# The opening of a one-core transformer layer: other fills on GpSimd, half of the queries cleared by ScalarE, the first products ordered by parts

## Chip, core and metric

The kernel runs on one core of one Trainium2 chip. The metric is the device time of one execution in microseconds (us), the median over several runs. A core has five engines with instruction streams of their own, which meet only at semaphores: TensorE (PE in the rows; its weight loads are PEld), VectorE (DVE), ScalarE (ACT), GpSimd (POOL) and SyncE (SP), which here only issues transfers.

## What is computed

The reference is a layer with two halves over `x` of 8 batches by 512 tokens by 256 channels. Cut to what the opening touches, it is:

```
xn = layernorm(x)                                  # rows: (x - mean) / sqrt(var + eps)
q, k, v = split(xn @ w_qkv.T)                      # 16 heads of 16
s = softmax(q @ k.T / 4 + causal) @ v @ w_out.T
g = silu((silu(xn @ wg.T) * (xn @ wu.T)) @ wd.T)   # 768 hidden columns
x = x + s * g
# second half: layernorm, a long convolution, a mixture of 20 experts, and x = x + s * silu(y)
```

## The kernel before, in words

Everything is one program with the order of each engine's work written out by hand and semaphores between the engines. The first half of the layer runs batch by batch (`sequence(b)` on every engine): batches 1 to 6 are a loop, batch 0 and the last are written out. Ahead of batch 0 stands the opening, the only place that the change touches: weights are loaded and converted, tiles that need constants are filled, batch 0 is normalised, projected and taken half-way through its gated hidden layer.

Products are made nearly exact with numbers cut in two parts, a high one (`HI`, rounded) and a low one (`LO`, what was lost). ScalarE writes the high part, VectorE or GpSimd subtracts it from the number and writes the low part. A projection is six products for each 128 output columns: three pairs of parts (`PAIRS`) by two halves of the 256 channels (`c`).

In the opening the engines do this:

- SyncE (`load_x`, `load_weights`) issues the loads of `x`, of the weights and of small tables, then `load_x(1)` when batch 0 is normalised, then writes the parts of queries and keys to memory (`spill`) and reads them back in the layout of the attention (`stack`, four groups of four heads). `stack` waits until the tiles `qs` and `ks` of its group have been filled.
- VectorE fills `nothing` and two of four groups of `qs` with zeros (`clear_queries`), does the first normalisation (`norm(0, NORM_X)`: statistics, variance, and in `norm_rows` four row tiles of `xn`), writes the low parts of `Wqkv` and of `xnT`, converts `Wgu`, writes the low parts of queries and keys (`split_qk`) with the other two clears between them, writes the low part of `Wg1`, multiplies the first three (`EARLY`) blocks of the hidden layer (`gated`), and does the second normalisation, `norm(1, NORM_X)`, for batch 1. Then it enters `sequence(0)`, which begins with `gated(0, 3)`.
- GpSimd builds masks, fills the four groups of `ks` with zeros and `V` with ones, and sets two rows of each group of `ks` to one (L1852). Between the second and the third group it raises the variance to the power of -1/2 (`power`), on which the rows of `xn` wait.
- TensorE transposes `xn` (L831), makes the four query and key tiles (`project_qk`, products at L822), the gate and up products of blocks 0 and 1 (`gate_up`), the values (`project_v`), block 2, and in `sequence(0)` blocks 3 to 5, batch 1's transposes, the down products (`down`, L904) and the scores (`unit`, L999). The gate and up products of block 3 wait for `v_sb` (the values kept), those of blocks 4 and 5 for `gated` of blocks 2 and 3.
- ScalarE converts weights, writes the high parts, and for each hidden block takes the SiLU of the gate (`silu_of_gate`, tile `sil`) and the high part of the product (`hidden`); GpSimd writes the low part of that product (`hidden_low`). `keep_v` copies the values into `V`.

The two lines that matter most for the order on VectorE ahead of `gated(0, 3)` and on TensorE ahead of block 5:

```
elif i >= 4:
    pe.wait_ge(S["h32_sb"], NF * b + i - 1)      # gate_up: block 5 waits for gated(0, 3)
...
norm(1, NORM_X)                                   # VectorE, then sequence(0): gated(0, 3)
```

Of the kernel before, what the change touches and what calls it, by code (L numbers as in the profile page):

```python
# [54 lines left out]
def program(nc, x, wqkvT, woutT, wguT, wdT, wg1, bg1, wg2, bg2, winT, bin_, short, wo2, bo2, fw1, fb1, fw2, fb2,  # L55
# [15 lines left out]
    with ctx:  # L71
# [210 lines left out]
        def f(ap):  # L282

            return ap.bitcast(F32)
# [295 lines left out]
        rest_in = sem("rest_in"); w_ms = sem("w_ms"); k_zero = sem("k_zero"); k_set = sem("k_set"); q_zero = sem("q_zero")  # L580
# [84 lines left out]
        def attention_sync(sp):  # L665
# [116 lines left out]
            for g in range(NG):  # L782
                sp.wait_ge(k_set, g + 1)
                sp.wait_ge(q_zero, g + 2)
                stack(0, g)
# [29 lines left out]
        def attention_tensor(pe):  # L815
# [18 lines left out]
            def project_qk(b, tiles):  # L834

                for m in tiles:
                    if m == 0:
                        pe.wait_ge(S["xnT_hi"], b + 1)
                        pe.wait_ge(S["xnT_lo"], b + 1)
                        at_least(pe, S["g_sb"], 2 * b)  # L840
                    if m >= 2:
                        pe.wait_ge(S["qk_lo"], 4 * b + m - 1)
                    o = C * (m % 2) + P * (m // 2)
                    split_products(PS[:, m % 2, :],
                                   lambda i, c: Wqkv[:, i, c, o:o + P],
                                   lambda j, c: xnT[:, j, c, :]).then_inc(S["qk_ps"], 1)

# [318 lines left out]
            pe.wait_ge(qkv_lo, 1)  # L1166
            project_qk(0, range(4))
# [27 lines left out]
        def attention_scalar(act):  # L1195
# [5 lines left out]
            def split_qk(b):  # L1201
                for m in range(4):
                    if m == 0:
                        at_least(act, S["on_sb"], NT * (b - 1))
                        at_least(act, S["ont"], b - 1)
                    act.wait_ge(S["qk_ps"], 4 * b + m + 1)
                    dst = khl if m % 2 else qhl
                    act.activation(dst[:, m // 2, HI, :], PS[:, m % 2, :], ACT.Copy).then_inc(S["qk_hi"], 1)
# [147 lines left out]

            act.wait_ge(qkv_in, 16)
            act.activation(Wqkv[:, HI, :, :], st_qkv[:, :, :], ACT.Copy).then_inc(qkv_hi, 1)
            split_x(0)
            act.wait_ge(d_in, 16)  # L1360
            act.activation(Wd[:, :, :], st_d[:, :, :], ACT.Copy).then_inc(d_sb, 1)
            split_qk(0)
            act.wait_ge(g1_in, 16)
# [3 lines left out]
            for i in range(EARLY):  # L1367
                if i == 0:
                    act.wait_ge(gu_sb, 1)
                    act.wait_ge(qkv_lo, 1)  # L1370
                    act.wait_ge(g1_lo, 1)
                silu_of_gate(0, i)
                hidden(0, i)
            act.wait_ge(v_ones, 1)
            act.wait_ge(rest_in, REST)
            keep_v(0)
# [17 lines left out]
        def attention_vector(dve):  # L1394
# [350 lines left out]
            split_qk(0, (0,))  # L1745
            clear_queries(2)
            split_qk(0, (1,))
            clear_queries(3)
            split_qk(0, (2, 3))
# [3 lines left out]
            for i in range(EARLY):  # L1753
                gated(0, i)
# [21 lines left out]
        def attention_gpsimd(pool):  # L1776
# [58 lines left out]

            pool.memset(neghalf[:, :], -0.5)
            pool.memset(mask16[:, :], 0.0).then_inc(w_ms, 1)
# [6 lines left out]
            for g in range(NG):  # L1844
                if g == 2:
                    power(0, veps, rstd, "ln_var", "ln_std")
                pool.memset(f(ks[:, GH * g:GH * g + GH, :]), 0.0).then_inc(k_zero, 1)
            pool.memset(V[:, :, :, :], 1.0).then_inc(v_ones, 1)
            pool.wait_ge(k_zero, NG)
            pool.wait_ge(v_ones, 1)  # L1850
            for g in range(NG):
                pool.memset(f(ks[M0:M0 + 2, GH * g:GH * g + GH, :]), 1.0).then_inc(k_set, 1)  # L1852
            pool.wait_ge(k_set, NG)
# [439 lines left out]
```

## Time and profile before

| | us |
|---|---|
| median of 3 runs | 1057.13 |
| lowest and highest run | 1054.28 and 1058.62 |
| span of the profiled execution, first to last instruction | 1027.7 |
| median less span | 29.4 |
| busy in the span: PE / DVE / ACT / POOL | 939.8 / 699.9 / 464.7 / 350.3 |
| mean granted TensorE clock (1.00 is 2.4 GHz, 0.50 is 1.2 GHz) | 0.968 |

The profiled execution has no time of its own beside its span; the 29.4 us between its span and the median of the runs lie before the first and behind the last instruction. All times below count from the first instruction of the span. TensorE is busy for 91% of the span, but does nothing in its first 19.7 us; the opening, up to the first scores of batch 0, takes the first 57 us.

### The profile page before, as it was taken

How to read it: one execution, taken by the hardware profiler on the slowest of the kernel's cores; microseconds unless marked ns; L12 is line 12 of the kernel's file. 1: busy time of each engine (PE TensorE's matmuls, PEld its weight loads, DVE VectorE, ACT ScalarE, POOL GpSimd, SP SyncE). 2: the span in 40 equal slices, each digit the busy share in tenths (PEclk: the TensorE clock that was granted, in tenths of full speed). 3: DMA queues.
4: the chain of work that ended last, by engine and by line, in shares of the span. 5: the costliest groups of instructions: out<-in, count | busy, mean ns of one | idle time of the engine just before them, and what ended most of it. 6: DMA issues, size and time to landing. Idle time of an engine off the chain costs nothing.

```text
span 1027.7 us, 18869 instructions
## 1 busy us (share of the span) xinstructions
PE 939.8 (91%) x5808; PEld 713.4 (69%) x5808; DVE 699.9 (68%) x1451; ACT 464.7 (45%) x869; POOL 350.3 (34%) x609
## 2 busy tenths in 40 slices
PE   1999999999999999999999999985798998999996
PEld 1776776776776686686686676564566677888885
DVE  8565477577577677667667566545375437999998
ACT  2435546546536636636636644633232334443441
POOL 7203313613623622532532451343000018833320
PEclk9988999999999999999999998988899999999999
DMA  5774854644634633733634630067767653544421
GB/s 184 157 159 80 161 190 66 123 150 80 115 133 96 117 139 87 117 131 91 104 115 112 103 128 22 2 217 224 253 218 229 212 185 115 164 129 141 144 86 41
DMA packets 88186, 136.68 MB, mean 133 GB/s; under 512 B 9987, under 2 KB 63939, under 8 KB 86084
## 3 DMA queue, kind: packets, MB, share of 16 engines
q1 hardware_dynamic: 69636, 100.75, 40.2%
q10 hardware_dynamic: 12352, 18.48, 5.3%
q0 software_dynamic: 6144, 16.79, 5.3%
q8 instruction: 27, 0.44, 0.2%
q14 instruction: 27, 0.22, 0.1%
HBM read 79.36 MB, written 55.57 MB: 131 GB/s over the span
## 4 chain that ended last, share of the span: by engine, by line
PE 38%; issue 29%; POOL 15%; DVE 10%; ACT 3%; DMA 2%; SPq 1%; POOLq 0%; DVEq 0%; ACTq 0%
PE PS L1980 7%; POOL PT L1800 6%; POOL slots_in L661 4%; PE PS L314 4%; PE PS L822 4%; PE PS L370 3%; PE PS L999 3%; POOL h L1783 3%; PE PS L1027 3%; PE PS L1041 3%; PE PS L337 2%; PE PS L405 2%; PE PS L1963 2%; POOL idle_p L1794 2%; DVE xn L1426 1%
## 5 line engine op out<-in xcount | busy, mean ns | idle before, releaser
L1510 DVE TENSOR_REDUCE Mneg<-PS 128x2 f32<-128x1024 f32 (+2 forms) x192 | 195.1, 1043 | 66.0 <-PE PS L1003 64.8
L1270 ACT ACTIVATE PT<-PS 128x512 f32<-128x512 f32 (+1 forms) x384 | 172.6, 529 | 118.1 <-PE PS L1027 116.2
L1794 POOL TENSOR_TENSOR idle_p<-neghalf 128x1 f32<-128x1 f32 x128 | 25.2, 197 | 304.0 <-ACT PT L1270 304.0
L999 PE MATMUL PS<-ks,qs 96*128 96x256 f32 (+3 forms) x512 | 121.5, 347 | 3.1 <-issue 2.1
L1027 PE MATMUL PS<-qs,ks 96*128 96x512 f32 (+3 forms) x512 | 121.1, 355 | 2.4 <-ACT PT L1270 1.3
L1027 PEld LDWEIGHTS PS<-qs,ks 96*128 96x128 f32 x512 | 88.1, 193 | 36.2 <-ACT PT L1270 18.1
L822 PE MATMUL PS<-xnT,Wgu 128*128 128x512 f32 x384 | 102.9, 409 | 2.9 <-ACT V L1215 2.4
L1980 PE MATMUL PS<-Wes,xbT 128*128 x336 | 99.0, 405 | 3.3 <-issue 2.6
L1800 POOL TENSOR_SCALAR_AFFINE_SELECT PT<-PT 128x256 f32<-128x256 f32 x256 | 99.0, 410 | 0.0
L1041 PE MATMUL PS<-PT,V 128*32 128x512 f32 (+3 forms) x1024 | 89.1, 455 | 5.4 <-POOL PT L1800 4.3
L822 PEld LDWEIGHTS PS<-xnT,Wgu 128*128 128x128 f32 x384 | 69.9, 191 | 25.8 <-issue 7.2
L999 PEld LDWEIGHTS PS<-ks,qs 96*128 96x128 f32 x512 | 77.5, 197 | 14.5 <-issue 9.1
L2203 POOL DMA_INDIRECT yg<-slots_out,pos x64 | 77.9, 1217 | 18.9 <-issue 17.9
L2038 DVE TENSOR_TENSOR yb<-PS,bes 128x256 f32<-128x256 f32 x84 | 35.2, 423 | 61.1 <-PE PS L1980 47.7
L1783 POOL TENSOR_TENSOR h<-h,h 128x512 fp32r<-128x512 f32 x40 | 51.3, 1290 | 62.0 <-ACT h L1234 61.8
L2002 ACT ACTIVATE xbT<-PS 128x256 f32<-128x256 f32 x84 | 31.4, 384 | 87.2 <-PE PS L1963 67.5
L1980 PEld LDWEIGHTS PS<-Wes,xbT 128*128 128x128 f32 x336 | 54.0, 196 | 23.4 <-issue 20.4
L661 POOL DMA_INDIRECT slots_in<-xn,rows_now x64 | 62.4, 974 | 17.5 <-issue 17.0
L1453 DVE SCALAR_TENSOR_TENSOR h<-PS,sil 128x512 f32<-128x512 f32 x48 | 32.5, 688 | 47.7 <-ACT sil L1227 36.4
L370 PE MATMUL PS<-Inv,Z 128*128 128x256 f32 x256 | 61.0, 393 | 3.0 <-DVE Z L519 2.5
L1003 PE MATMUL PS<-mask,ident 128*128 128x128 f16 (+2 forms) x352 | 63.6, 256 | 0.0
L314 PE MATMUL PS<-v,Fwd 128*128 128x256 f32 x432 | 57.1, 293 | 2.8 <-issue 2.8
(233 smaller groups left out, 1600.3 us busy)
## 6 DMA issues: line engine op xcount, KB each, us to landing
qs<-qk_parts SPq DMA_DIRECT2D x96, 128.0 KB
ks<-qk_parts SPq DMA_DIRECT2D x96, 128.0 KB
slots_out<-yb ACTq DMA_DIRECT2D x28, 384.0 KB, 3.1
xb<-slots_in SPq DMA_DIRECT2D x83, 128.0 KB, 2.6
qk_parts<-qhl SPq DMA_DIRECT2D x16, 512.0 KB, 2.7
qk_parts<-khl SPq DMA_DIRECT2D x16, 512.0 KB, 3.1
xn2T_parts<-xn2T SPq DMA_DIRECT2D x8, 1024.0 KB, 4.9
xT<-xn2T_parts ACTq DMA_DIRECT2D x7, 1024.0 KB
```

Of the source, the lines that this page charges most:

```text
L314: last = pe.matmul(PS[:, bank, C * (q_ % 2):C * (q_ % 2) + C], Fwd[:, i, kc, P * q_:P * q_ + P], src[:, j, 2 * half + kc, :], start=n == 0 ...
L370: last = pe.matmul(PS[:, 6 + m, C * z:C * z + C], Z[:, z, c, P * m:P * m + P], Inv[:, c, :], start=c == 0, stop=c == NQ - 1)
L661: pool.indirect_dma_start(slots_in, bass.IndirectOffsetOnAxis(rows_now[:, t, k:k + 1], axis=0), xn2[:, t, :], None).then_inc(S["sent"], 16)
L822: last = pe.matmul(out, lhs(i, c), rhs(j, c), start=last is None, stop=n == 0)
L999: pe.matmul(out, qs[:, hd, P * qt:P * qt + P], ks[:, hd, 0:keys], start=n % a_bank == 0, stop=False, skip_group_check=True)
L1027: last = pe.matmul(PS[:, 4 + n, col:col + T - P * kt], ks[:, hd, P * kt:P * kt + P], qs[:, hd, P * kt:T], start=True, stop=True)
L1041: last = pe.matmul(PS[32 * j:32 * j + 32, 7, P * kt:T], V[:, kt, GH * g + j, :], PT[:, g % 2, j, COL[kt]:COL[kt] + T - P * kt], start=kt = ...
L1270: act.activation(PT[:, g % 2, j, 512 * n:512 * n + width], PS[:, 4 + n, 0:width], ACT.Exp, scale=SCALE).then_inc(S["exped"], 1)
L1510: dve.tensor_reduce(out=Mneg[:, 0, qt, heads[0]:heads[-1] + 1], in_=all_of, op=ALU.max, axis=AX.X, negate=True).then_inc(S["maxed"], 1)
L1783: pool.tensor_tensor(h[:, i, LO, :], h32[:, i % 2, :], f(h[:, i, HI, :]), ALU.subtract).then_inc(S["h_lo"], 1)
L1800: last = pool.affine_select(out=blocks, in_=blocks, compare_op=ALU.is_ge, fill=0.0, base=0, pattern=[[0, 2], [1, P]], channel_multiplier=-1)
L1980: ins = pe.matmul(PS[:, HALF + u % HALF, 0:C], xbT[:, u, c, :], Wes[:, bass.ds(expert, 1), c, :].rearrange("p o n -> p (o n)"), start=c == ...
```

## The change

It leaves the arithmetic as it is and changes only which engine fills which tile, in which order, and the order of the six products of each of batch 0's query and key tiles.

- GpSimd: a group of `ks` is filled with ones at once (`keys_of_ones`) in the place of a fill with zeros and a second one of two rows with ones; the rows between are multiplied by zeros of `qs`. Two groups come first, then `power`, then a wait until all four row tiles of `xn` are written, and only then the other two groups, `V` and the masks.
- ScalarE clears groups 2 and 3 of `qs` at its very start; VectorE no longer does.
- TensorE's first four tiles use `project_qk_first`: high by high first, then low weights by high `xnT`, then high weights by low `xnT`, each with a wait of its own.
- ScalarE's order: the conversion of `Wd` goes from ahead of the query and key splits to behind `keep_v`; `keep_v` goes ahead of block 2; the high part of `Wg1` and `ident16` go behind the three early blocks. VectorE's low part of `Wg1` goes behind them too.

```
@@ attention_sync
-                sp.wait_ge(k_set, g + 1)
-                sp.wait_ge(q_zero, g + 2)
+                sp.wait_ge(k_ones, g + 1)
+                if g < 2:
+                    sp.wait_ge(q_zero, g + 2)
+                else:
+                    sp.wait_ge(q_cleared, g - 1)
                 stack(0, g)
@@ attention_tensor
+            def project_qk_first(m):
+                o = C * (m % 2) + P * (m // 2)
+                if m >= 2:
+                    pe.wait_ge(S["qk_lo"], m - 1)
+                n = 0
+                for i, j in ((HI, HI), (LO, HI), (HI, LO)):
+                    if m == 0 and i == j:
+                        pe.wait_ge(S["xnT_hi"], 1)
+                        pe.wait_ge(qkv_hi, 1)
+                    if m == 0 and i == LO:
+                        pe.wait_ge(qkv_lo, 1)
+                    if m == 0 and j == LO:
+                        pe.wait_ge(S["xnT_lo"], 1)
+                    for c in range(CC):
+                        last = pe.matmul(PS[:, m % 2, :], Wqkv[:, i, c, o:o + P], xnT[:, j, c, :],
+                                         start=n == 0, stop=n == 5)
+                        n += 1
+                last.then_inc(S["qk_ps"], 1)
...
-            pe.wait_ge(qkv_lo, 1)
-            project_qk(0, range(4))
+            for m in range(4):
+                project_qk_first(m)
@@ attention_scalar
+            act.wait_ge(q_zero, 1)
+            for g in (2, 3):
+                act.activation(qs[:, GH * g:GH * g + GH, :].rearrange("p h t -> p (h t)"),
+                               nothing[0:KS, 0:1].to_broadcast([KS, GH * T]), ACT.Copy).then_inc(q_cleared, 1)
             act.wait_ge(qkv_in, 16)
             act.activation(Wqkv[:, HI, :, :], st_qkv[:, :, :], ACT.Copy).then_inc(qkv_hi, 1)
             split_x(0)
-            act.wait_ge(d_in, 16)
-            act.activation(Wd[:, :, :], st_d[:, :, :], ACT.Copy).then_inc(d_sb, 1)
             split_qk(0)
+            for i in range(EARLY):
+                if i == 0:
+                    act.wait_ge(gu_sb, 1)
+                    act.wait_ge(qkv_lo, 1)
+                if i == 2:
+                    act.wait_ge(v_ones, 1)
+                    keep_v(0)
+                    act.wait_ge(d_in, 16)
+                    act.activation(Wd[:, :, :], st_d[:, :, :], ACT.Copy).then_inc(d_sb, 1)
+                    act.wait_ge(d_sb, 1)
+                silu_of_gate(0, i)
+                hidden(0, i)
             act.wait_ge(g1_in, 16)
             act.activation(Wg1[:, HI, :, :], st_g1[:, :, :], ACT.Copy).then_inc(g1_hi, 1)
...
-            for i in range(EARLY):
-                if i == 0:
-                    act.wait_ge(gu_sb, 1)
-                    act.wait_ge(qkv_lo, 1)
-                    act.wait_ge(g1_lo, 1)
-                silu_of_gate(0, i)
-                hidden(0, i)
-            act.wait_ge(v_ones, 1)
+            act.wait_ge(g1_lo, 1)
             act.wait_ge(rest_in, REST)
-            keep_v(0)
@@ attention_vector
-            split_qk(0, (0,))
-            clear_queries(2)
-            split_qk(0, (1,))
-            clear_queries(3)
-            split_qk(0, (2, 3))
+            split_qk(0, range(4))
+            for i in range(EARLY):
+                gated(0, i)
             dve.wait_ge(g1_hi, 1)
             dve.tensor_tensor(Wg1[:, LO, :, :], st_g1[:, :, :], f(Wg1[:, HI, :, :]), ALU.subtract
                               ).then_inc(g1_lo, 1)
-            for i in range(EARLY):
-                gated(0, i)
             norm(1, NORM_X)
@@ attention_gpsimd
+            def keys_of_ones(g):
+                pool.memset(f(ks[:, GH * g:GH * g + GH, :]), 1.0).then_inc(k_ones, 1)
             pool.memset(neghalf[:, :], -0.5)
+            keys_of_ones(0)
+            keys_of_ones(1)
+            pool.wait_ge(k_ones, 2)
+            power(0, veps, rstd, "ln_var", "ln_std")
+            pool.wait_ge(S["ln_done"], NT)
+            keys_of_ones(2)
+            keys_of_ones(3)
+            pool.memset(V[:, :, :, :], 1.0).then_inc(v_ones, 1)
             pool.memset(mask16[:, :], 0.0).then_inc(w_ms, 1)
...
-            for g in range(NG):
-                if g == 2:
-                    power(0, veps, rstd, "ln_var", "ln_std")
-                pool.memset(f(ks[:, GH * g:GH * g + GH, :]), 0.0).then_inc(k_zero, 1)
-            pool.memset(V[:, :, :, :], 1.0).then_inc(v_ones, 1)
-            pool.wait_ge(k_zero, NG)
-            pool.wait_ge(v_ones, 1)
-            for g in range(NG):
-                pool.memset(f(ks[M0:M0 + 2, GH * g:GH * g + GH, :]), 1.0).then_inc(k_set, 1)
-            pool.wait_ge(k_set, NG)
             for i in range(EARLY):
                 hidden_low(0, i)
```

GpSimd's stream from the end of the masks to the first low part of a hidden block, before (`TENSOR_TENSOR rstd` is `power`):

```order
L1842 AFFINE_SELECT mask_68<-mask_68 128x128
L1847 MEMSET ks 96x2048 x2
L1779 TENSOR_TENSOR rstd<-veps,neghalf 128x4 [waits s_ln_var]
L1847 MEMSET ks 96x2048 x2
L1848 MEMSET V 128x2048
L1852 MEMSET ks 2x2048 [waits v_ones,k_zero]
L1852 MEMSET ks 2x2048 x3
L1783 TENSOR_TENSOR h<-h_116,h 128x512 [waits s_h_hi,k_set]
```

and GpSimd's stream in the changed kernel, from its first instruction of the opening into the masks:

```order
L1865 MEMSET neghalf 128x4
L1863 MEMSET ks 96x2048 x2
L1804 ISA
L1804 TENSOR_TENSOR rstd<-veps,neghalf 128x4 [waits s_ln_var,k_ones]
L1863 MEMSET ks 96x2048 [waits s_ln_done]
L1863 MEMSET ks 96x2048
L1873 MEMSET V 128x2048
L1874 MEMSET mask_68 128x128
L1875 MEMSET ones_66 128x128
```

The two groups of `ks` that stood right behind `power` now wait for `s_ln_done`, and the four fills of two rows are gone.

ScalarE's stream behind the third query and key tile, before (`khl` is the fourth tile's high part, `Wg` is `Wg1`, `sil` the SiLU, `h<-h` the high part of a hidden block):

```order
L1208 ACTIVATE khl<-PS 128x512 [waits s_qk_ps]
L1364 ACTIVATE Wg_88<-st_g_121 128x256 [waits g1_in]
L1366 ACTIVATE ident_67<-ident 128x128 [waits ident_in]
L1227 ACT_TABLE_LOAD [waits g1_lo,s_gu_ps,qkv_lo]
L1227 ACTIVATE sil<-PS 128x512 [waits gu_sb]
L1234 ACTIVATE h<-h_116 128x512 [waits s_h32_sb]
L1227 ACTIVATE sil<-PS 128x512 [waits s_gu_ps]
L1234 ACTIVATE h<-h_116 128x512 [waits s_h32_sb]
L1227 ACTIVATE sil<-PS 128x512 [waits s_h32_sb,s_gu_ps]
L1234 ACTIVATE h<-h_116 128x512 [waits s_h32_sb]
L1215 ACTIVATE V<-PS 128x32x16 [waits s_v_ps,rest_in,v_ones]
L1215 ACTIVATE V<-PS 128x32x16 [waits s_v_ps]
```

and in the changed kernel:

```order
L1231 ACTIVATE khl<-PS 128x512 [waits s_qk_ps]
L1250 ACT_TABLE_LOAD [waits s_gu_ps,qkv_lo]
L1250 ACTIVATE sil<-PS 128x512 [waits gu_sb]
L1257 ACTIVATE h<-h_116 128x512 [waits s_h32_sb]
L1250 ACTIVATE sil<-PS 128x512 [waits s_gu_ps]
L1257 ACTIVATE h<-h_116 128x512 [waits s_h32_sb]
L1238 ACTIVATE V<-PS 128x32x16 [waits s_v_ps,v_ones]
L1238 ACTIVATE V<-PS 128x32x16 [waits s_v_ps]
L1396 ACTIVATE Wd<-st_d 128x1536 [waits d_in]
L1250 ACTIVATE sil<-PS 128x512 [waits s_h32_sb,s_gu_ps,d_sb]
L1257 ACTIVATE h<-h_116 128x512 [waits s_h32_sb]
L1401 ACTIVATE Wg_88<-st_g_121 128x256 [waits g1_in]
```

The load of the SiLU's table no longer waits for `g1_lo`; `V` and `Wd` stand ahead of the third `sil`, and `Wg` behind the third `h`.

VectorE's stream between the split of the fourth tile and the rows of batch 1's normalisation, before (`h<-PS,sil` is `gated`, `stats` begins `norm(1, NORM_X)`):

```order
L1443 TENSOR_TENSOR khl<-PS,khl 128x512 [waits s_qk_hi]
L1751 TENSOR_TENSOR Wg_88<-st_g_121,Wg_88 128x256 [waits g1_hi]
L1453 SCALAR_TENSOR_TENSOR h_116<-PS,sil 128x512 [waits s_silu_sb,s_gu_ps] x2
L1453 SCALAR_TENSOR_TENSOR h_116<-PS,sil 128x512 [waits s_h_hi,s_h_lo,s_silu_sb,s_gu_ps]
L1407 BN_STATS stats<-xin 128x6 [waits s_x_in]
L1407 BN_STATS stats<-xin 128x6 x3
```

and in the changed kernel:

```order
L1472 TENSOR_TENSOR khl<-PS,khl 128x512 [waits s_qk_hi]
L1482 SCALAR_TENSOR_TENSOR h_116<-PS,sil 128x512 [waits s_silu_sb,s_gu_ps] x2
L1482 SCALAR_TENSOR_TENSOR h_116<-PS,sil 128x512 [waits s_h_hi,s_h_lo,s_silu_sb,s_gu_ps]
L1778 TENSOR_TENSOR Wg_88<-st_g_121,Wg_88 128x256 [waits g1_hi]
L1436 BN_STATS stats<-xin 128x6 [waits s_x_in]
L1436 BN_STATS stats<-xin 128x6 x3
```

The low part of `Wg1` now stands between the third `gated` and the normalisation of batch 1, and the normalisation still stands ahead of the fourth `gated`.

## Rows read from the trace of the kernel before

**Rows 1.** Waits of PE up to 62 us: total, times, longest.

```profile
PE PS L831 <- DVE xn L1426: 19.8, 1, 19.8
PE PS L822 <- DVE xnT L1436: 2.5, 1, 2.5
PE PS L822 <- ACT V L1215: 2.4, 1, 2.4
```

**Rows 2.** Timeline, fills and normalisations: start us, us, engine, line, operation, [idle before].

```profile
6.54 1.48 ACT L1358 ACTIVATE Wqkv<-st_qkv 128x1536 fp32r<-128x1536 f32 x1 [4.43 <-DMA st_qkv<-wqkvT]
...
8.48 3.54 POOL L1847 MEMSET ks<- 96x2048 f32 x2
...
8.54 11.07 DVE L1426 TENSOR_SCALAR xn<-xin,mv,rstd 128x256 f32<-128x256 f32 x4 [1.17 <-POOL rstd L1779]
...
11.97 1.79 POOL L1848 MEMSET V<- 128x2048 f32 x1
...
13.88 7.47 POOL L1852 MEMSET ks<- 2x2048 f32 x4
...
19.54 1.74 DVE L1740 TENSOR_TENSOR Wqkv<-st_qkv,Wqkv 128x1536 fp32r<-128x1536 f32 x1
...
45.22 1.38 DVE L1426 TENSOR_SCALAR xn<-xin,mv,rstd 128x256 f32<-128x256 f32 x4 [1.21 <-POOL rstd L1779]
```

**Rows 3.** Timeline, from the transposed rows to block 2.

```profile
21.74 1.02 ACT L1199 ACTIVATE xnT<-PS 128x1024 fp32r<-128x1024 f32 x1 [13.72 <-PE PS L831]
...
22.79 1.23 DVE L1436 TENSOR_TENSOR xnT<-PS,xnT 128x1024 fp32r<-128x1024 f32 x1 [1.52 <-ACT xnT L1199]
...
23.93 1.75 DVE L1744 CAST Wgu<-st_gu 128x3072 fp32r<-128x3072 int32 x1
...
24.16 8.65 PE L822 MATMUL PS<-xnT,Wqkv 128*128 128x512 f32 x24 [2.46 <-DVE xnT L1436]
...
29.66 0.60 ACT L1208 ACTIVATE khl<-PS 128x512 fp32r<-128x512 f32 x1 [1.96 <-PE PS L822]
...
39.24 2.00 PE L822 MATMUL PS<-xnT,Wgu 128*128 128x512 f32 x8
```

**Rows 4.** Timeline, early blocks and the second normalisation.

```profile
34.30 0.41 DVE L1751 TENSOR_TENSOR Wg<-st_g,Wg 128x256 fp32r<-128x256 f32 x1
...
34.87 1.28 ACT L1227 ACT_TABLE_LOAD   x1 [0.92 <-DVE Wg L1751]
...
39.56 0.63 ACT L1234 ACTIVATE h<-h 128x512 fp32r<-128x512 f32 x1 [0.83 <-DVE h L1453]
...
41.89 1.39 DVE L1407 BATCH_NORM_STATS2 stats<-xin 128x6 f32<-128x256 f32 x4
...
42.54 1.07 ACT L1215 ACTIVATE V<-PS 128x512 f32<-128x512 f32 x2
...
46.60 0.17 DVE L1758 TENSOR_SCALAR next_row<-ramp 128x20 f32<-128x20 f32 x1
...
47.20 0.69 DVE L1453 SCALAR_TENSOR_TENSOR h<-PS,sil 128x512 f32<-128x512 f32 x1 [0.43 <-PE PS L822]
```

**Rows 5.** Timeline, an addition on VectorE without and beside GpSimd.

```profile
126.74 1.23 DVE L1612 TENSOR_TENSOR xres<-xres,G 128x1024 f32<-128x1024 f32 x1
...
204.83 1.31 POOL L1783 TENSOR_TENSOR h<-h,h 128x512 fp32r<-128x512 f32 x1
...
205.10 2.14 DVE L1612 TENSOR_TENSOR xres<-xres,G 128x1024 f32<-128x1024 f32 x1
```

**Rows 6.** Timeline of PE from block 3 to the down products.

```profile
43.66 7.17 PE L822 MATMUL PS<-xnT,Wgu 128*128 128x512 f32 x24 [2.42 <-ACT V L1215]
...
51.46 5.90 PE L904 MATMUL PS<-Wd,h 128*128 128x256 f32 x48
```

**Rows 7.** Stretches: engines' busy us (instructions), PEclk, DMA share, GB/s.

```profile
43.70:46.60 2.90, 2.90 (x7) 2.34 (x8) 1.66 (x8) 0.60 (x1) 1.30 (x2) 0.50 1.07 128
70.70:84.10 13.40, 13.28 (x52) 9.19 (x55) 7.93 (x11) 6.73 (x13) 3.62 (x12) 0.50 0.66 219
```

More of the change, by code:

```diff
@@ L579, in program @@
         qkv_in = sem("qkv_in"); ident_in = sem("ident_in"); gu_in = sem("gu_in"); d_in = sem("d_in"); g1_in = sem("g1_in")
-        rest_in = sem("rest_in"); w_ms = sem("w_ms"); k_zero = sem("k_zero"); k_set = sem("k_set"); q_zero = sem("q_zero")
+        rest_in = sem("rest_in"); w_ms = sem("w_ms"); k_ones = sem("k_ones"); q_zero = sem("q_zero"); q_cleared = sem("q_cleared")
         v_ones = sem("v_ones"); qkv_hi = sem("qkv_hi"); qkv_lo = sem("qkv_lo"); g1_hi = sem("g1_hi"); g1_lo = sem("g1_lo")
```

## The prediction

> **What bounds it now.** I read the waits of TensorE in the opening first, since TensorE is the engine with the most work. Up to 62 us there are three [rows 1]: 19.8 us for the rows of the first normalisation, 2.5 us for the low part of `xnT`, 2.4 us for the kept values `V`. The list has no wait for a split of queries or keys. All later work of the run hangs behind these products, so a microsecond gained up to the down products is gained at the end, if nothing else comes late.
>
> Then the timeline says why the first wait is so long. The four row tiles of `xn` take 11.07 us, where the same four for batch 1 take 1.38 us [rows 2]. In the slow stretch, 8.54 to 19.61, GpSimd fills without a break: two groups of `ks`, `V`, four pairs of rows, up to 21.35. At 45.22 it fills nothing. The low part of `Wqkv`, 1536 columns in 1.74 us, ran beside the last of these fills at some 1.1 ns a column, no more than the 1.2 ns that the low part of `xnT` took after the fills (1.23 us for 1024) [rows 2, 3]. So fills hold up the row tiles and not such subtractions.
>
> **The change part by part.** The profiled execution spans 1027.7 us; the median of the runs, 1057.13, is 29.4 above it. I work in times of the span and take the difference off the median.
>
> *Rows of `xn`.* GpSimd now does nothing between `power` and the fourth row tile. From 8.54 the rows take 1.38 and end at 9.92 in the place of 19.61: 9.7 us gained. Lowest case: the fills are not the cause, gain 0.
>
> *Order by parts.* Before, the first product began at 24.16 behind the low part of `xnT`, which ended at 24.02; the high part ended at 22.76 [rows 3]. Now the first product waits for the high part alone: 1.26 us earlier. The third product needs `Wqkv`'s low part (9.92 plus 1.74, 11.7) and the fifth `xnT`'s (24.02 less 9.69, 14.3). The first product starts at 24.16 - 9.69 - 1.26 = 13.2, and the first twelve took 5.50 us, 0.46 each [rows 3], so these are needed at 14.1 and 15.0: no wait.
>
> *Clears on ScalarE.* Two times 2048 columns at the rate of 1536 in 1.48 make 3.9 us, an estimate; ScalarE had 4.43 us idle ahead of that conversion [rows 2]. Cost nothing. Were they twice as long, the high part of `Wqkv` would end near 12, still ahead of 13.2. Taking two clears from VectorE gives nothing either, as no wait of TensorE of any length hangs on the splits behind them [rows 1].
>
> *The fills that are left.* Two groups of `ks` and `V` run from 9.95 for 3.54 + 1.79, to 15.3, and four narrow ones follow, of 128 columns against the 2048 of `V`, together at most one more `V` fill: 17.1. The conversion of `Wgu` wants to start at 14.35 and may be held like the row tiles. If it waits for all, it ends at 17.1 + 1.75 = 18.85; the first block's products need it at 13.2 + 8.65 = 21.9. The split of the first query tile stands behind it (another 0.7, to 19.55), and the third tile's products wait for that split; they are due at 13.2 + 5.5 = 18.7. Bounds 0 to 0.85 us of loss; I take 0, since narrow fills end sooner and the conversion has until 18.0 to be done. Here the Trainium skill speaks against the change ("SBUF — State Buffer", Who interferes with whom): a cast in the two-port mode and a GpSimd instruction exclude each other, for the whole instruction. By it the conversion waits for the fill under way, to 15.3, and nothing is lost; but the first row tile of `xn` in this trace was held across several fills, which is the 0.85 case.
>
> *ScalarE's chain of hidden blocks.* The load of the SiLU's table waited for `Wg1`'s low part until 34.87 [rows 4]. Now it waits for the first gate product alone. Block 0 starts at 21.9, half of its eight products (2.00 us for eight [rows 3]) are done at 22.9. From the table load to the end of block 1's high part it was 34.87 to 40.19, 5.3 us: now 28.2. `V` follows, 1.07: 29.3 (its products end where block 2 began, 39.24 - 24.16 = 15.1 after the first product, 28.3). Then `Wd`, which has the 1536 columns of the conversion at 6.54, 1.48: 30.75. SiLU 0.6 (a tile of 512 columns, as `khl` [rows 3]), `gated` 0.69, high part 0.63 and three hand-overs give `gated` of block 2 at 32.2 and its high part at 32.9.
>
> *What comes late next: the second normalisation.* VectorE now waits for `Wg1`'s high part (0.4 behind 32.9), then takes its low part, then does `norm(1)` and two small rows, 41.89 to 46.77, 4.88 us [rows 4], and only then `gated` of block 3. `Wg1`'s low part has both its inputs in SBUF, and meets GpSimd's subtraction for block 2, which starts at 32.95 and takes 1.31. An addition of the same kind took 1.23 with GpSimd idle and 2.14 beside that subtraction, ending 1.1 behind it [rows 5]. So the low part ends at 34.25 + 0.4 = 34.65 (33.8 if not held). The fourth `gated` starts at 39.6 and ends at 40.3; before it started at 47.20. Of the 10.9 gained at the first product 7.6 are left.
>
> *TensorE.* The wait for `V` is gone: block 2 ends at 41.24 - 24.16 = 17.1 behind the first product, at 30.3, and `V` is there at 29.3. Blocks 3 and 4 take 4.0 and end at 34.3. Block 5 needs the fourth `gated`: a pause of 6.0 us. Behind the pause of 2.4 us before, TensorE ran at a granted clock of 0.50, 1.2 GHz, for at least 2.9 us, seven products [rows 7]. Block 5's eight at that rate take 3.3 and end at 43.6; before, block 5 ended at 50.83 [rows 6]. From there to the end of the down products it was 6.5 us, to 57.36 [rows 6]: now 50.1 at the full clock, 50.6 with the half clock for another microsecond, as I take it. Lowest case as in the stretch from 70.7, where 0.50 lasted 13.4 us [rows 7]: until 53.7, so that 10.1 us behind block 5 do the work of 5.05, and the end is at 55.2.
>
> *Sum.* 9.7 + 1.3 (rows and order) + 2.4 (wait for `V`) - 6.0 (new pause) - 0.2 (blocks 3 to 5 take 4.0 + 3.3 in the place of 7.17, and rounding) - 0.5 (clock behind block 5) = 6.7 us; the same from the ends, 57.36 - 50.6 = 6.8. Behind it come the scores and the same sequences as before; the stacked queries and keys, written and read back by SyncE, start earlier by as much as the splits, some 11 us, so the scores find them. Predicted: 1057.13 - 6.7 = **1050.4 us**.
>
> **The rivals.**
>
> *The half clock stays.* The new pause is longer than the old one, and the trace has both kinds of stretch behind a pause [rows 7]. With 13.4 us the gain is 57.36 - 55.2 = 2.2: 1054.9. Against it: behind the pause here come products without waits, as at 43.7; at 70.7 to 84.1 the scores come in pieces. The Trainium skill ("TensorE: Matmul & The Clock Gate", Part 1) has the half clock as the default that sustained work lifts; by that the loss ends within the stretch's first products, 0 to 0.5, and the time is 1050. The trace agrees at 43.7; that TensorE was busy 13.28 of 13.40 us at 0.50 [rows 7] does not fit, so the rival keeps its chance.
>
> *The half clock stays away later.* The stretch at 70.7 is not tied to the opening's work but to what TensorE did just before. Shifted, it may fall out. At most half of 13.4 comes back, 6.7; TensorE waits for others there too, so half of that: 3.4 more, 1047.0.
>
> *The fills are not the cause.* The row tiles stay at 11 us, for instance because the weights arrive in the same stretch. Then only the order changes: 6.7 - 9.7 = -3.0, that is 1060.1. Against it: the subtraction of `Wqkv` and the tiles at 45.22.
>
> *Slower.* The same clock, but through the first batch's attention: half speed from the pause at 34 on until after 70, where the run before had 13.4 us of it. Each microsecond more can cost up to 0.5; the gain of 6.7 is gone after 13.4 us more at full price, and 5.3 slower is reached after 24 more. It would give some 1063. Nothing in the trace shows so long a stretch.
>
> **How the numbers follow.** The forecast, 4.5 to 9 us gained, gets 0.62; the staying half clock 0.15; the lucky clock 0.12; fills not the cause 0.07; slower 0.04. The forecast's own range is 1048 to 1052.6. The range for 8 in 10 takes in the lucky clock's side and the staying half clock: 1045.5 to 1055. A measurement of this kernel tells 0.5%, 5.3 us, from no change. Faster by more than that: five sixths of the forecast (0.52) and the lucky clock, 0.64, with a little of the staying clock 0.66. Slower: 0.04. The rest, 0.30, within.
>
> **What would show it.** Right: the four row tiles of `xn` in about 1.4 us; the first transposes near 10 and first products near 13.2; no wait for `V`, but one of about 6 us behind block 4, put down to the fourth `gated`; `Wg1`'s low part at 1 us or more; half clock on block 5; the scores 6 to 8 us earlier. Wrong: row tiles above 3 us; a wait of TensorE among its first 24 products; `gated` of block 3 much before or behind 39.6; or the scores earlier by as much as said and the end not, which would put the difference into the clock of batch 0's attention.

## The result and the profile after

The changed kernel takes 1042.78 us (median of 20 runs, 1038.31 to 1052.23), the kernel before 1053.07 (20 runs, 1043.12 to 1062.32). The ratio is 0.9933, with a 95% interval of 0.9905 to 0.9960: 7.1 us gained of 1053, between 4.2 and 10.0. The forecast was 6.7 us. The two medians lie further apart, 10.3 us, and why the two figures differ stays open; a later run of the same kernel, below, gives 10.5 by the ratio. The forecast of 1050.4 stands on a median before of 1057.13, from three runs; over 20 runs it is 1053.07, so gains are compared here and not end times.

The profiled execution of the changed kernel has a span of 1043.0 us and a time of its own of 1044.7, so that only 1.7 us lie outside a span. The 29.4 us that the table of before puts outside the span are therefore not there. The execution of before that the prediction read, with its span of 1027.7, was an unusually short one (the fastest of the 20 runs before took 1043.12), and ends cannot be compared between the two. The openings can.

The waits of TensorE up to 62 us, after (total, times, longest):

```profile
PE PS L834 <- DVE xn L1455: 10.1, 1, 10.1
PE PS L825 <- DVE h L1482: 5.5, 1, 5.5
PE PS L866 <- ACT xnT L1222: 1.1, 1, 1.1
PE PS L1022 <- issue: 1.0, 1, 1.0
PE PS L1034 <- DVE Mparts L1550: 0.4, 1, 0.4
```

Against [rows 1] the first wait has lost 9.6 us (it ended at 19.76 and ends at 10.14), the second, now for the high part of `xnT`, has gone from 2.5 to 1.1 us, the wait for `V` is gone, and a wait of 5.5 us for the fourth `gated` (L1482) is new. The timeline of the same stretch, after:

```profile
2.12 3.71 ACT L1382 ACTIVATE qs<-nothing 96x2048 fp32r<-96x2048 f32 x2
6.43 1.48 ACT L1385 ACTIVATE Wqkv<-st_qkv 128x1536 fp32r<-128x1536 f32 x1 [0.61 <-DMA st_qkv<-wqkvT]
...
8.61 1.38 DVE L1455 TENSOR_SCALAR xn<-xin,mv,rstd 128x256 f32<-128x256 f32 x4 [1.24 <-POOL rstd L1804]
9.91 1.75 DVE L1769 TENSOR_TENSOR Wqkv<-st_qkv,Wqkv 128x1536 fp32r<-128x1536 f32 x1
10.05 3.54 POOL L1863 MEMSET ks<- 96x2048 f32 x2 [1.48 <-DVE xn L1455]
...
13.19 8.13 PE L866 MATMUL PS<-xnT,Wqkv 128*128 128x512 f32 x24 [1.11 <-ACT xnT L1222]
13.54 1.80 POOL L1873 MEMSET V<- 128x2048 f32 x1
14.31 2.64 DVE L1773 CAST Wgu<-st_gu 128x3072 fp32r<-128x3072 int32 x1
15.28 1.81 POOL L1874 MEMSET mask<- 128x128 f16 x1
...
22.36 1.28 ACT L1250 ACT_TABLE_LOAD   x1 [0.40 <-PE PS L825]
...
27.57 1.07 ACT L1238 ACTIVATE V<-PS 128x512 f32<-128x512 f32 x2
28.53 1.49 ACT L1396 ACTIVATE Wd<-st_d 128x1536 fp32r<-128x1536 int32 x1
...
32.17 1.29 POOL L1808 TENSOR_TENSOR h<-h,h 128x512 fp32r<-128x512 f32 x1 [3.12 <-ACT h L1257]
32.43 1.31 DVE L1778 TENSOR_TENSOR Wg<-st_g,Wg 128x256 fp32r<-128x256 f32 x1 [1.00 <-ACT Wg L1401]
33.66 1.39 DVE L1436 BATCH_NORM_STATS2 stats<-xin 128x6 f32<-128x256 f32 x4
...
38.32 0.69 DVE L1482 SCALAR_TENSOR_TENSOR h<-PS,sil 128x512 f32<-128x512 f32 x1
39.06 3.78 PE L825 MATMUL PS<-xnT,Wgu 128*128 128x512 f32 x8 [5.47 <-DVE h L1482]
44.20 6.22 PE L927 MATMUL PS<-Wd,h 128*128 128x256 f32 x48
50.26 0.63 PE L1022 MATMUL PS<-ks,qs 96*128 96x512 f32 x2
```

The four row tiles of `xn` take 1.38 us in the place of 11.07 [rows 2], the first product starts at 13.19 in the place of 24.16 [rows 3], the down products end at 50.42 in the place of 57.36 [rows 6]. Stretches, after (us, busy us of PE, PEld, DVE, ACT and POOL with instructions, PEclk, DMA share, GB/s):

```profile
39.00:42.80 3.80, 3.74 (x9) 2.86 (x10) 0.70 (x2) 2.23 (x4) 2.40 (x2) 0.50 1.07 132
42.80:44.80 2.00, 2.00 (x12) 2.00 (x11) 1.23 (x2) 0.84 (x2) 0.15 (x1) 0.50 1.07 117
44.80:50.20 5.40, 5.40 (x47) 5.40 (x47) 1.38 (x2) 1.41 (x2) 0.00 (x0) 0.99 0.86 109
...
62.00:84.00 22.00, 20.51 (x146) 12.92 (x146) 16.42 (x22) 12.46 (x26) 7.24 (x24) 1.00 0.71 193
...
221.00:231.00 10.00, 9.88 (x44) 8.37 (x44) 5.82 (x9) 5.23 (x13) 2.72 (x9) 0.57 0.07 28
231.00:236.00 5.00, 5.00 (x22) 1.96 (x25) 3.33 (x6) 0.36 (x2) 0.90 (x3) 0.50 0.32 70
```

Behind the new pause TensorE has the half clock (0.50, 1.2 GHz) to 44.8. The 13.4 us at 0.50 in batch 0's attention [rows 7] are not there, but a like stretch stands from 221 to 236.

### The profile page after: what moved, and what is told of

Read it like the earlier page. It is cut to its first block, busy times and chain, and to the rows that moved or that the text cites. A ratio compares the mean times of both kernels' runs of the same rounds, so it can differ in the third digit from the quotient of the medians.

```text
span 1043.0 us, 18864 instructions
## 1 busy us (share of the span) xinstructions
PE 947.2 (91%) x5808; PEld 714.8 (69%) x5808; DVE 686.1 (66%) x1449; ACT 467.5 (45%) x871; POOL 327.1 (31%) x605
## 3 DMA queue, kind: packets, MB, share of 16 engines
q10 hardware_dynamic: 12352, 18.48, 5.3%
## 4 chain that ended last, share of the span: by engine, by line
PE 33%; issue 31%; POOL 13%; DVE 12%; ACT 3%; DMA 1%; another core or an unknown queue 1%; SPq 1%; POOLq 0%; DVEq 0%; ACTq 0%
PE PS L2007 8%; POOL PT L1825 6%; PE PS L1050 3%; PE PS L370 3%; POOL slots_in L661 3%; PE PS L1064 3%; PE PS L1022 3%; DVE tmp L478 3%; POOL h L1808 3%; PE PS L825 3%; PE PS L314 2%; PE PS L1990 2%; POOL idle_p L1819 2%; PE PS L337 1%; DVE tmq L478 1%
## 5 line engine op out<-in xcount | busy, mean ns | idle before, releaser
L314 PE MATMUL PS<-v,Fwd 128*128 128x256 f32 x432 | 59.5, 297 | 8.8 <-issue 8.7
L2230 POOL DMA_INDIRECT yg<-slots_out,pos x64 | 61.0, 954 | 18.5 <-issue 17.7
L1482 DVE SCALAR_TENSOR_TENSOR h<-PS,sil 128x512 f32<-128x512 f32 x48 | 32.5, 688 | 49.5 <-ACT sil L1250 38.4
L314 PEld LDWEIGHTS PS<-v,Fwd 128*128 128x128 f32 x432 | 56.5, 203 | 11.0 <-issue 9.6
```

The lines of the kernel that those rows point to most:

```text
L314: last = pe.matmul(PS[:, bank, C * (q_ % 2):C * (q_ % 2) + C], Fwd[:, i, kc, P * q_:P * q_ + P], src[:, j, 2 * half + kc, :], start=n == 0 ...
```

## The experiments

They ran on three chips: the fills alone, the fills back, the old product order and `Wd` early on one (before: 1054.26 there); the normalisation between the blocks with its variant, the padding and the kernel before on another (1057.07); the wait between the fills and the last two on a third (1053.31). Each ratio is against the kernel before on the same chip. "Scores" is the start of batch 0's first scores: 57.19 before, 50.26 after.

**Only the fills.** The kernel before with GpSimd's part of the change alone:

```
 pool.memset(neghalf[:, :], -0.5)
+keys_of_ones(0); keys_of_ones(1); pool.wait_ge(k_ones, 2)
+power(0, veps, rstd, "ln_var", "ln_std")
+pool.wait_ge(S["ln_done"], NT)
+keys_of_ones(2); keys_of_ones(3)
+pool.memset(V[:, :, :, :], 1.0).then_inc(v_ones, 1)
...
-for g in range(NG): ...        # the old fills, power between them
```

> The kernel before with GpSimd's part of the change alone: merged fills, two groups ahead of power, the rest behind the four row tiles of xn; SyncE waits for the merged fills. ScalarE, VectorE and the order of products stay as before. Theory (fills held the row tiles; the new order on ScalarE and VectorE costs time again): row tiles in 1.4 us, first product at 24.16 - 9.7 = 14.5, the whole opening 9.7 earlier with the wait for V still there, first scores at 57.2 - 9.7 = 47.5, that is about 2.8 us earlier than the full change has them (50.26). Rival (the other parts of the change help or cost nothing): first scores at 50.3 or later. Third possibility, fills not the cause: row tiles stay above 5 us.

1042.81 us, ratio 0.9900 (0.9864 to 0.9936). The rows take 1.38 us, the first product starts at 14.54, the wait for `V` is still 2.4 us (L1215), but there is no pause for the fourth `gated`:

```profile
PE PS L831 <- DVE xn L1426: 10.1, 1, 10.1
PE PS L822 <- DVE xnT L1436: 2.5, 1, 2.5
PE PS L822 <- ACT V L1215: 2.4, 1, 2.4
```

Scores at 47.56. So the fills alone bring 9.6 us at the scores, and the rest of the change takes 2.7 of them back: it removes the wait for `V` and makes the pause. That the rest also costs time at the end is not shown: the fills alone gain 10.5 us there, the whole change 7.1 and 10.5. VectorE's lines with the fills alone, ahead of the fourth `gated`:

```profile
32.29 1.40 DVE L1407 BATCH_NORM_STATS2 stats<-xin 128x6 f32<-128x256 f32 x4
...
37.56 0.69 DVE L1453 SCALAR_TENSOR_TENSOR h<-PS,sil 128x512 f32<-128x512 f32 x1 [0.41 <-PE PS L822]
```

The fourth `gated` comes earlier here than in the whole change (38.32), though the first product is 1.35 later: the second normalisation begins right behind the third `gated` (which starts at 31.68), while in the whole change 1.00 us of waiting for `Wg1`'s high part and the 1.31 of its low part stand between the two.

**Fills back in the normalisation.** The changed kernel less one line:

```
 power(0, veps, rstd, "ln_var", "ln_std")
-pool.wait_ge(S["ln_done"], NT)
 keys_of_ones(2)
```

> The changed kernel without GpSimd's wait for the four row tiles: the second half of the fills starts right behind power, beside the row tiles. Theory (fills hold the row tiles, and fills back to back keep them out): the first row tile ends only when the fills of ks and V are through, near 14, the other three soon after, so row tiles of 5 to 7 us in the place of 1.38, first product 4 to 6 us later than 13.19, at 17 to 19, and first scores at 54 to 56 in the place of 50.26. Rival (transfers into the core's memory hold the row tiles): row tiles 1.4 us, scores at 50.3.

1048.2 us, 0.9956 (0.9924 to 0.9988); scores at 55.56, first product at 18.48, as the theory had it. The fills beside the rows, and the row tiles of `xn` (durations in ns, shortest, median, longest; first and last start):

```profile
8.55 3.54 POOL L1863 MEMSET ks<- 96x2048 f32 x2
8.61 6.67 DVE L1455 TENSOR_SCALAR xn<-xin,mv,rstd 128x256 f32<-128x256 f32 x4 [1.24 <-POOL rstd L1804]
...
12.04 1.79 POOL L1872 MEMSET V<- 128x2048 f32 x1
13.78 0.19 POOL L1873 MEMSET mask<- 128x128 f16 x1
13.93 0.19 POOL L1874 MEMSET ones<- 128x128 f16 x1
```

```profile
L1455 DVE TENSOR_SCALAR xn<-xin,mv,rstd x4: 399/420/5659, 8.6 to 14.9; 128x256 f32<-128x256 f32 x4
```

One tile took 5.66 us, from 8.61 to 14.27, past three fills of 1.77 to 1.79 us and the two short ones behind them; the other three took 0.4 each. The fills are the cause.

**A wait between the fills.** The same, with GpSimd waiting for each fill:

```
 keys_of_ones(2)
+pool.wait_ge(k_ones, 3)
 keys_of_ones(3)
+pool.wait_ge(k_ones, 4)
 pool.memset(V[:, :, :, :], 1.0).then_inc(v_ones, 1)
+pool.wait_ge(v_ones, 1)
```

> The changed kernel with the fills back inside the first normalisation, as in the run with the fills put back, but GpSimd waits for the end of each fill before it issues the next. Theory (a fill that stands ready behind the one under way keeps VectorE's row tile out, and a wait between them lets it in): the first row tile ends at 10.4 to 11.2 in place of 14.27, all four by 16 at the latest, the first product at 15 to 18 in place of 18.48. Rival (only the whole run of fills matters, a wait of a few hundredths changes nothing): first row tile at 13.9 to 14.4 again and the first product at 18.3 or later.

```profile
8.54 3.68 POOL L1863 MEMSET ks<- 96x2048 f32 x2
8.61 6.09 DVE L1455 TENSOR_SCALAR xn<-xin,mv,rstd 128x256 f32<-128x256 f32 x4 [1.24 <-POOL rstd L1804]
...
12.29 1.83 POOL L1874 MEMSET V<- 128x2048 f32 x1
```

```profile
L1455 DVE TENSOR_SCALAR xn<-xin,mv,rstd x4: 512/1922/1966, 8.6 to 14.2; 128x256 f32<-128x256 f32 x4
```

No tile is held across fills now: three take 1.9 us, one fill each, the fourth 0.5; all end at 14.70, and the first product starts at 17.89 in the place of 18.48 (one time, 1050.11 us). Each gap lets one tile in, and the next fill holds the next tile. So here it is the fill standing ready behind the one under way that kept VectorE out; a conversion that got in without a gap is told of below.

**Old product order.**

```
-for m in range(4):
-    project_qk_first(m)
+pe.wait_ge(qkv_lo, 1)
+project_qk(0, range(4))
```

> The changed kernel with the first products in their old order and behind both low parts. Theory: first product 1.2 us later, at 14.4 behind the low part of xnT, all later stations of the opening as much later, first scores at 51.5. Rival (the wait hides in a later one): first scores at 50.3, with the first product at 14.4.

1043.45 us, 0.9896 (0.9855 to 0.9936). First product at 14.54, 1.35 later; the 24 products take 7.60 us in the place of 8.13, the fourth `gated` comes at 39.13, 0.81 later, the scores at 50.60, 0.34 later. The unchanged after, run again below, has its scores at 50.77: at the scores the gain is inside the scatter, nearer to the rival than to the theory. The 24 products differ by their spacing: the first start 0.43 us or more apart, the later ones mostly 0.23. Here seven of these gaps are long, in the changed kernel ten, and eight and 13 in the two runs with the moved normalisation on the second chip, which order them as the changed kernel does; what sets the number was not tried.

**`Wd` early again.**

```
 act.activation(Wqkv[:, HI, :, :], st_qkv[:, :, :], ACT.Copy).then_inc(qkv_hi, 1)
 split_x(0)
+act.wait_ge(d_in, 16)
+act.activation(Wd[:, :, :], st_d[:, :, :], ACT.Copy).then_inc(d_sb, 1)
 split_qk(0)
...
     keep_v(0)
-    (the same two lines, and a wait for d_sb)
```

> The changed kernel with the conversion of Wd back where it was, behind the high part of xnT and ahead of the splits. There ScalarE idles 3.0 us in the changed kernel (13.13 to 16.15), and the conversion takes 1.49. Theory (ScalarE's chain sets the fourth gated, on which TensorE pauses): the third gated and so the fourth are 1.5 us earlier, pause of TensorE ahead of block 5 near 4.0 in the place of 5.5, first scores at 48.8. Rival (something else, as the second normalisation's own inputs, sets it): first scores at 50.3.

1042.72 us, 0.9896 (0.9859 to 0.9933); pause 4.8 us in the place of the 4.0 expected, scores at 48.49, near the 48.8 expected, but by another sum. The fourth `gated` comes only 0.64 earlier (37.68), since the third now waits for TensorE's product; the rest is clock: the stretch from 38.4 to 41.8 has a PEclk of 0.58 and block 5 takes 3.38 us in the place of 3.78, and from its end to the end of the down products it is 6.85 us in the place of 7.58. At the end of the run no gain over the changed kernel is shown.

**The second normalisation between the blocks.** The changed kernel with

```
-for i in range(EARLY):
-    gated(0, i)
+gated(0, 0)
+gated(0, 1)
+norm_stats(1, NORM_X)
+norm_variance(1, NORM_X)
+gated(0, 2)
+norm_rows(1, NORM_X)
 dve.wait_ge(g1_hi, 1)
 (Wg1's low part)
-norm(1, NORM_X)
...
@@ GpSimd
 hidden_low(0, 0); hidden_low(0, 1)
+power(1, veps, rstd, "ln_var", "ln_std")
 hidden_low(0, 2)
-power(1, veps, rstd, "ln_var", "ln_std")
```

> The changed kernel, but the second normalisation's statistics stand between the second and the third gated product of VectorE, its rows behind the third, ahead of Wg1's low part; GpSimd takes the power between the second and third low parts of the hidden values. Theory (TensorE's 5.5 us pause comes from the normalisation that now stands between Wg1's low part and the fourth gated product): the fourth gated product starts at 34.7 to 35.3 in place of 38.32, the pause ahead of block 5 shrinks to 0 to 2 us, and the first scores come at 46 to 47.2 in place of 50.26. Rival (ScalarE's chain of three conversions and Wg1 sets the fourth gated product, and the normalisation lies in its shadow): the fourth gated product stays above 37.5 and the scores within 1 us of 50.26. In the time: if every microsecond at the scores reaches the end, 3 to 4 us below the changed kernel, some 1039; if the clock of the later stretches decides, 1042 to 1043 as in the other variants.

1043.15 us, 0.9859 (0.9806 to 0.9912); the changed kernel with padding (below), on the same chip, had 1050.29. Waits of PE, timeline and a stretch:

```profile
PE PS L825 <- DVE h L1482: 1.9, 1, 1.9
```

```profile
33.23 0.41 DVE L1782 TENSOR_TENSOR Wg<-st_g,Wg 128x256 fp32r<-128x256 f32 x1
33.68 0.60 ACT L1250 ACTIVATE sil<-PS 128x512 f32<-128x512 f32 x1 [1.47 <-DVE Wg L1782]
34.36 0.69 DVE L1482 SCALAR_TENSOR_TENSOR h<-PS,sil 128x512 f32<-128x512 f32 x1 [0.56 <-issue]
35.11 2.11 PE L825 MATMUL PS<-xnT,Wgu 128*128 128x512 f32 x8 [1.90 <-DVE h L1482]
...
43.82 0.63 PE L1022 MATMUL PS<-ks,qs 96*128 96x512 f32 x2
```

```profile
35.00:38.00 3.00, 2.89 (x17) 2.33 (x17) 0.74 (x2) 2.10 (x4) 1.57 (x2) 1.00 1.07 126
```

The fourth `gated` comes 4.0 us earlier and the scores 6.4: the pause shrinks by 3.6, and block 5 behind it runs at the full clock, 2.11 us in the place of 3.78. The expectation of 46 to 47.2 was too late: it allowed 3.1 to 4.3 us, little more than the 3.0 to 3.6 it gave the fourth `gated`, and the full clock brought 1.7 on block 5 and 0.8 behind it besides. Even so the rows of the normalisation now meet GpSimd's low part and take 2.35 us in the place of 1.38.

**The same with `Wd` early.** Both edits together.

> As the run before, and Wd's conversion stands ahead of the splits again, as in the kernel before. Theory: V and the third SiLU come 1.5 us earlier, so the fourth gated product starts at 33.3 to 34.5, TensorE has no pause over 1 us ahead of block 5, block 5 runs at full clock (2.0 us for eight products), and the first scores come at 45 to 46.2. Rival (the third gated product waits for TensorE's own products, as when Wd alone was put back): the fourth gated product comes only 0 to 0.6 us earlier than in the run before, and the scores within 0.7 us of it. Time: 1038 to 1042.

1044.75 us, 0.9873 (0.9820 to 0.9926); fourth `gated` at 34.13, scores at 43.60: 0.2 us earlier than without `Wd`, as the rival had it. The pause is 1.2 us, and the expected time of 1038 to 1042 was missed.

**Padding ScalarE's stream.** Six activations of one column at its start:

```
+PAD = 6
...
-idle_a = keep("idle_a", [P, 1])
+idle_a = keep("idle_a", [P, 8])
...
 act.wait_ge(q_zero, 1)
+for n in range(PAD):
+    act.activation(idle_a[:, 1 + n:2 + n], nothing[:, 0:1], ACT.Copy)
...
```

> The changed kernel with six activations of one column more at the very start of ScalarE's stream, which hide behind its idle time there. It tests the 0.65 us by which ScalarE's last copy of an output tile comes later behind its product in each of the six loop iterations (1.46 us idle ahead of it in place of 0.84). Theory (where the loop's code lies in ScalarE's stream sets it): another figure than 1.46, as 0.84, and the loop's iterations at 48.0 to 48.1 us in place of 48.6 to 48.9. Rival (the position has nothing to do with it): 1.4 to 1.5 again, the iterations at 48.6 or more, and the time within 0.5% of the changed kernel.

1050.29 us, 0.9931 (0.9895 to 0.9967), scores at 50.00. ScalarE's idle time ahead of its last copy of an output tile is 1.50 to 1.59 us in five of the six iterations, 1.32 in the sixth: the rival. What the expectations call an iteration is a part of it, from the fourth row of maxima of one batch to the first of the next (L1035 here); it takes 49.7 to 49.8 us. A whole iteration, first row to first row, takes 80.5 to 80.7.

**The kernel before, once more.**

> The kernel before, profiled once more, to see what belongs to its one shown execution. Theory (the 0.84 us ahead of ScalarE's last copy and the late part without stalls of TensorE belong to that execution): 1.4 to 1.5 us here, and a span of 1040 to 1060. Rival (they belong to the kernel): 0.84 again, iterations of 48.0 to 48.1 us, and a span near 1027.7. In both the opening as shown: the first product at 24.2, the first scores at 57.2.

Time 1056.85, span 1055.1. The opening is as shown: first product at 24.17, scores at 57.39. The idle time is 1.47 to 1.59 us in the first five iterations and the part of an iteration told of above takes 48.9 to 49.9, so the short ones belonged to the execution shown. So did the late part. Waits of PE from 640 us, here and then in the execution first shown:

```profile
PE PS L314 <- issue: 17.7, 13, 2.8
```

```profile
PE PS L314 <- issue: 2.8, 1, 2.8
```

**After and the moved normalisation on one chip.**

> The changed kernel again, beside the run after it on the same chip. Theory (what differs between executions of one program is the loop's iterations, 48.0 to 49.8 us, and the late part, and not the opening): first product at 13.19, first scores at 50.2 to 50.3 again, the iterations anywhere from 48.0 to 49.8, the time 0.989 to 0.996 of the kernel before. Rival (the opening varies too): scores more than 0.5 us off 50.26.

> The changed kernel with the second normalisation between the gated products, on the same chip as the changed kernel. Theory (6.4 us at the first scores reach the end): 4 to 9 us below the changed kernel of this call, 0.980 to 0.991 of the kernel before. Rival (the time is set behind the opening, as the 1042 to 1043 of all variants of the first call lets one think): within 2 us of the changed kernel of this call.

After: 1043.66 us, 0.9900 (0.9867 to 0.9933), first product at 13.20, scores at 50.77, 0.51 us later than in the first profile, so that by a hair the rival holds: the opening varies too. Its 24 first products took 8.45 us in the place of 8.13. The moved normalisation: 1038.35 us, 0.9863 (0.9822 to 0.9903), scores at 44.05. By the medians it is 5.3 us ahead of the changed kernel, by the ratios 3.9, with scores 6.7 earlier; the intervals overlap from 0.9867 to 0.9903, so that it beats the kernel before is shown, and its lead over the changed kernel only likely.

What the runs gave at the scores (against 57.19) and at the end, the gain being one minus the ratio, times the median of before on that chip:

| kernel | earlier at the scores | gain at the end |
|---|---|---|
| fills back in | 1.6 | 4.6 (1.3 to 8.0) |
| after, again | 6.4 | 10.5 (7.1 to 14.0) |
| after with padding | 7.2 | 7.3 (3.5 to 11.1) |
| after, first result | 6.9 | 7.1 (4.2 to 10.0) |
| old product order | 6.6 | 11.0 (6.7 to 15.3) |
| `Wd` early | 8.7 | 11.0 (7.1 to 14.9) |
| fills only | 9.6 | 10.5 (6.7 to 14.3) |
| normalisation between | 13.4 | 14.9 (9.3 to 20.5) |
| the same with `Wd` early | 13.6 | 13.4 (7.8 to 19.0) |
| normalisation between, third chip | 13.1 | 14.4 (10.2 to 18.7) |

In eight of the ten rows the gain at the scores lies within the interval of the gain at the end, in two (after again, old product order) the end gained more. So what the opening gains arrives, as far as intervals of some 6 to 11 us can show it; differences of 2 or 3 us between rows they cannot show.

## Why the prediction was right, and where its steps were off

*The rows of `xn`.* Forecast 9.7 us, measured 9.7 in their length and 9.6 at the first transposes; putting the fills back took 5.3 us away at the scores, and the fills alone gave 9.6. Shown. The mechanism is finer than the prediction's "fills hold up the row tiles": a tile was held across fills that followed each other without a gap, 5.66 us, and 1.9 us where there was one. The Trainium skill ("SBUF — State Buffer", Who interferes with whom) says that the second to issue is blocked until the first instruction has finished. By it the first tile would have ended near 10.7 without any gap (an estimate: the end of the first fill and 0.4 for the tile); the run shows 14.27, and the measurement decides. `Wgu`'s conversion in the changed kernel does agree with it: it starts at 14.31, takes 2.64 us where 1.75 were needed alone [rows 3], so 0.9 more, and `V`'s fill ended 1.0 after its start; the mask's fill behind it, 0.20 us elsewhere, then took 1.81. Why VectorE got in between these two fills and not between those of `ks` stays open.

*The conversion of `Wgu`.* Taken at no loss, bounds 0 to 0.85. It was held 0.9 us, done at 16.95, within its margin, and the list of TensorE's waits has none among its 24 first products.

*Order by parts.* Forecast 1.3, measured 1.35 at the first product, 0.81 at the fourth `gated`, and at the scores no more than the scatter. The term is right where it was read, at the first product, but does not last: the 24 products took 7.60 us when they began later, and between 7.77 and 8.55 in nine executions that order them as the changed kernel does.

*Clears on ScalarE.* Estimated 3.9 us at no cost. Measured 3.71, done 0.6 us before the weights arrived. Right.

*Low part of `Wg1` and the new pause.* The low part beside GpSimd's subtraction took 1.31 us, forecast 1.35; alone it was 0.41 [rows 4]. The fourth `gated` started at 38.32, forecast 39.6, because ScalarE's chain ran ahead of the reckoning: the first gate products began at 21.16, forecast 21.9, the table load came at 22.36, forecast 22.9, the third `gated` ended at 31.42, forecast 32.2, and `Wg1`'s low part at 33.74, forecast 34.65. The pause was 5.5 us, forecast 6.0. That the second normalisation makes most of it is shown by moving it: 1.9 is left. With the fills alone it stood in the same place without making a pause, as TensorE was still held by the wait for `V`; the 2.3 us of waiting and low part that the change put ahead of it were not tried by themselves.

*Half clock behind the pause.* Forecast: block 5 in 3.3 us and 0.5 us lost behind it. Measured 3.78, and 7.58 us from block 5's end to the end of the down products in the place of 6.53, so 1.05. Together 1.0 us too low, made up by block 5's start at 39.06, forecast 40.3: two misses that cancel, which is luck. With the pause at 1.9 us the half clock did not come and block 5 took 2.11.

*Sum.* Forecast 6.7 with the down products' end at 50.6; measured 50.42, so 6.9 there, and 7.1 us by the ratio. The agreement within 0.4 us is closer than the interval, 4.2 to 10.0, and the second figure, 10.5, allow one to claim. *Wrong was a statement beside the sum*, in the table of before: that 29.4 us lie outside the span. It is 1.7; the execution read was that much faster than the runs. The sum stood because it was made of differences.

*The rivals.* "Fills not the cause" fell with the fills put back. "The half clock stays" fell: it ended at 44.8. "The half clock stays away later" seemed to come true, since 62 to 84 is at full clock, but the stretch only wandered: after, it lies at 221 to 236 in one execution and nowhere in the other; before, it lies in batch 0 in one execution and nowhere in the other. "Slower" showed nowhere.

## What to carry to other kernels

Keep GpSimd's fills away from row-wise work of VectorE by a wait on that work, not only by their place in the stream; even a wait between fills lets single tiles through. When one wait in an opening is shortened, look at which long sequence now stands alone ahead of the next hand-over (here `Wg1`'s low part, which waits for ScalarE, and a normalisation of 4.7 us) and put it where the engine would be waiting anyway. What such a pause costs is its length and, behind the pause of 5.5 us, 2.7 us of half clock (block 5 took 1.67 more than the 2.11 behind 1.9 us, and 1.05 were lost behind it); behind pauses of 1.2 and 1.9 us the granted clock stayed at 1.00, behind 2.4 it was 0.50 [rows 7]; and a single profiled execution is good for its opening, not for its end.

## What had not been expected of the hardware

- A stretch at half clock wanders. In nine of thirteen profiled executions one batch's attention was 4.3 to 5.2 us longer between its first and third rows of maxima (L1011 before, L1034 after), though not the same: batch 0 in four, the first execution of before among them (24.3 us against 20.0; PEclk 0.50), batch 1 or 2 in two, the last batch in three; in four executions there is none, the second one of before among them. The two executions of the kernel before differ in it, and so do the two of the changed kernel, so it is not tied to the code.
- One unchanged part of the loop, from the fourth row of maxima of a batch to the first of the next, took 48.0 to 48.1 us in the execution first shown, 48.4 to 49.9 in the twelve others. Some 0.65 us of it is ScalarE's last copy of an output tile, which mostly starts 1.4 to 1.6 us after its last work in the place of 0.7 to 0.9; neither padding nor the change moves it. What sets it stays open.
- In the convolution TensorE issued single products about 1.4 us apart for some 20 us (863 to 882 in the second execution of before), waiting for nothing that the profile shows: such waits come to 17.7 us in all there, to 2.8 in the first. This scatter, ten microseconds and more, is larger than most of what the change moves, and its cause was not tried.
- A short fill of a mask, 0.20 us, took 1.81 when VectorE's conversion was under way: GpSimd can be the one that waits. With a wait between the fills one of its masks (L1879) took 1.88 us beside VectorE's subtraction for `Wqkv`, 0.29 in the changed kernel.
